# Gated delta stage: one table set for the norm's logarithm and exponential, a repeated identity product, key products behind the updates

## The reference

```python
q, k, v = causal_conv_silu(x @ Wq.T), causal_conv_silu(x @ Wk.T) * scale, causal_conv_silu(x @ Wv.T)
a, beta = sigmoid(x @ Wa.T + ba), sigmoid(x @ Wb.T + bb)
def step(S, (qt, kt, vt, at, bt)):            # one token
    err = einsum('bhij,bhj->bhi', S, kt) - vt
    S = at[..., None] * S - bt[..., None, None] * (err[..., None] * kt[:, :, None, :])
    o = einsum('bhij,bhj->bhi', S, qt)
o = scan(step, zeros, 512 tokens)
o = (o - mean(o)) / sqrt(var(o) + eps) * ln_w + ln_b      # per head
layer = (o * sigmoid(x @ Wg.T)) @ Wo.T
```

## Time and profile before

| | us |
|---|---|
| three runs | 2849.22, 2838.45, 2849.55 (median 2849.22) |
| the profiled execution, its own time | 2847.4 |
| its span (first to last instruction) | 2845.6 |
| VectorE busy in the span | 2072.3 (73%) |
| TensorE busy in the span | 2388.4 (84%) |
| ScalarE busy in the span | 1626.4 (57%) |
| mean granted TensorE clock | 0.923 of full speed |

### The profile page before, as it was taken

One profiled execution on the slowest core, in us unless ns is written; L12 is line 12 of the kernel. 1 busy time (PEld: TensorE's weight loads), 2 busy tenths in 40 slices (PEclk: granted clock), 3 DMA queues, 4 the chain that ended last, 5 costly groups with the idle time before them and its releaser, 6 DMA issues. The chain is left out here.

```text
span 2845.6 us, 63751 instructions
## 1 busy us (share of the span) xinstructions
PE 2388.4 (84%) x25649; PEld 1591.6 (56%) x25701; DVE 2072.3 (73%) x3811; ACT 1626.4 (57%) x4119; POOL 263.7 (9%) x278
## 2 busy tenths in 40 slices
PE   6788888877888788887994999999997886999777
PEld 5666666666667666664442666666642322332376
DVE  6889998889889889882123777778726775886465
ACT  3656677666666766665234777777641113667344
POOL 0000000000000000000011101100002342110342
PEclk9889999889999989998996999999998998999889
DMA  5110111111011111002006999999510003231422
GB/s 185 32 32 17 32 32 32 32 32 30 19 32 32 32 32 30 19 17 71 0 12 173 236 249 227 232 241 233 127 37 0 0 0 103 54 88 24 172 71 65
DMA packets 205726, 219.48 MB, mean 77 GB/s; under 512 B 32966, under 2 KB 191446, under 8 KB 199990
## 3 DMA queue, kind: packets, MB, share of 16 engines
q1 hardware_dynamic: 203033, 210.44, 28.3%
q0 software_dynamic: 2400, 4.95, 0.5%
HBM read 137.96 MB, written 79.79 MB: 77 GB/s over the span
## 5 line engine op out<-in xcount | busy, mean ns | idle before, releaser
L2871 DVE TENSOR_REDUCE dl_ZO<-dl_XP 128x64 f32<-128x128 f32 (+6 forms) x448 | 219.7, 490 | 15.5
L1990 ACT ACTIVATE da_AB<-ps 128x384 f32<-128x384 f32 x256 | 124.7, 491 | 140.8 <-PE ps L1851 137.1
L2866 DVE TENSOR_TENSOR dl_XP<-dl_ZO,dl_G 128x128 f32<-128x128 f32 (+5 forms) x384 | 177.0, 461 | 13.2
L2000 ACT ACTIVATE da_E<-ps,da_top 128x512 f32<-128x512 f32 x256 | 176.2, 688 | 17.2 <-DVE da_top L2146 16.7
L2143 DVE TENSOR_TENSOR ps<-ps,da_window 128x192 f32<-128x192 f32 (+1 forms) x256 | 101.3, 396 | 116.3 <-PE ps L1874 112.0
L1470 DVE TENSOR_REDUCE ra_top<-ps 128x1 f32<-128x512 f32 x256 | 159.2, 680 | 36.2 <-PE ps L1236 22.8
L2146 DVE TENSOR_REDUCE da_top<-ps 128x1 f32<-128x512 f32 x256 | 176.9, 691 | 8.8
L2450 PE MATMUL ps<-dl_ST,ident 128*128 128x512 f32 x256 | 139.3, 672 | 46.0 <-ACT dl_Q L2638 46.0
L1370 ACT ACTIVATE ra_PT<-ps 128x512 f32<-128x512 f32 x256 | 136.0, 601 | 61.0 <-PE ps L1267 59.1
L1881 PE MATMUL ps<-ident,da_E 128*128 128x128 f32 x1024 | 168.7, 288 | 1.6 <-ACT da_E L2000 1.5
L2384 PEld LDWEIGHTS ps<-X,dl_taps_v 128*128 128x128 f32 x1088 | 145.5, 216 | 18.2 <-issue 12.9
(11 more groups left out here) (411 smaller groups left out, 5855.9 us busy)
## 6 DMA issues: line engine op xcount, KB each, us to landing
da_bands<-da_AB SPq DMA_DIRECT2D x128, 384.0 KB, 3.8
dl_Abc<-dl_ends SPq DMA_DIRECT2D x64, 512.0 KB, 6.2
da_window<-da_bands SPq DMA_DIRECT2D x128, 192.0 KB, 4.4
da_across<-da_bands SPq DMA_DIRECT2D x128, 192.0 KB, 4.5
da_parts<-da_split SPq DMA_DIRECT2D x64, 96.0 KB, 3.4
ra_parts<-ra_split SPq DMA_DIRECT2D x16, 384.0 KB, 3.5
rf_We<-in_rf_We SPq DMA_DIRECT2D x1, 4608.0 KB, 24.1
da_K<-da_parts SPq DMA_DIRECT2D x16, 256.0 KB
```

The source lines that it names most:

```text
L1990: eng.activation(AB[:, j % STAGES, h, :, :], ps[:, band_bank(v), 0:2 * BAND].rearrange("p (k x) -> p k x", k=2), ACT.Copy)\
L2000: eng.activation(E[:, U % 2, :], ps[:, score_bank(U), :], ACT.Exp, bias=top[:, u:u + 1], accum_out=total[:, m % 2, u:u + 1]).then_inc(s["e ...
L2866: link(eng.tensor_tensor(XP[:, :, :, SB - t:], seen.unsqueeze(1).to_broadcast([P, 2, I, t + 1]), G[:, x:x + 2, keys][:, ::-1, :].unsqueeze ...
L2871: link(eng.tensor_reduce(ZO[:, to:to + 1 + (2 * I - 1) * CH:CH].rearrange("p (k i) -> p k i", k=2), XP[:, :, :, SB - 1 - t:], AXX, ALU.add))
```

## The change

Four edits in the delta stage. (1) `deviation` asks for one table set that has both functions, and stands ahead of the copy of the values' first half rather than behind it. (2) `kept(2)` is issued five times more ahead of itself; each overwrites bank 0 with the same quarter, so what is computed stays. (3) In the second half's boundary the products of `LAST_KEYS` stand behind the updates rather than ahead of them. (4) On VectorE `prepare(n + 1, 1)` stands ahead of `gate_keys` and `residual` rather than behind them.

```diff
+    REPEATS = 5
@@ TensorE
-            def kept(r):
-                eng.matmul(ps[:, UPDATES[r], :], c.ident[:, :], quarters[:, r, :, :], start=True, stop=False)
+            def kept(r, alone=False):
+                eng.matmul(ps[:, UPDATES[r], :], c.ident[:, :], quarters[:, r, :, :], start=True, stop=alone)
@@ boundary
                 eng.wait_ge(s["wc"], 6 * n + 3 * e + 3)
                 eng.sem_inc(c.past, 1)
+                for g, k, h, r in itertools.product(range(GR), range(2), range(2), range(GR)):
+                    update(g, k, h, r)
                 if e == 1:
                     key_products(LAST_KEYS).then_inc(s["g"], 1)
-                for g, k, h, r in itertools.product(range(GR), range(2), range(2), range(GR)):
-                    update(g, k, h, r)
                 for r in range(GR):
                     next_start(r)
@@ one_pass
                 eng.wait_ge(s["evac"], (n + 1) * PROJ + 3)
+                for _ in range(REPEATS):
+                    kept(2, True)
                 kept(2)
                 boundary(n, 0)
@@ ScalarE
             def deviation(n):
+                eng.preload_act_table_set("natural_log_exp_and_others")
                 eng.wait_ge(s["var"], n + 1)
@@ one_pass
-                evacuate(n + 1, 1, 3)
+                evacuate(n + 1, 1, 2)
                 if not first:
                     deviation(n - 1)
+                evacuate(n + 1, 2, 3)
                 boundary(n, 0)
@@ VectorE, one_pass
                 end(n, 1, first)
+                prepare(n + 1, 1)
                 gate_keys(n + 1)
                 if not first:
                     residual(n - 1)
-                prepare(n + 1, 1)
                 begin(n + 1, 0)
```

## The result

The changed kernel takes **2826.07 us** in the median of six runs (2822.43 to 2827.16), the kernel before 2850.22 in its six (2838.45 to 2855.65): ratio 0.9914 [0.9897, 0.9931]. The forecast was 2838, the likeliest case being no measurable change; it is faster by 0.9%. The profiled execution took 2825.35 with a span of 2823.6, 22.0 us shorter than the span before.

What follows compares the result with a forecast made beforehand. VectorE was taken as the busiest engine in the delta stage, so only its waits count. Against the profiled 2847.4: -13.0 + 2.0 + 0.9 - 1.3 = -11.4, so 2836.0, on the median 2838 us; range 2812 to 2862.

Steps and rivals of the forecast that it cites:

- the sum of the first halves: First halves of passes 1 to 15: nine products of 0.89 us up to the transposes, a loss of 2 us in all.
- I leave it unchanged: First halves, transposes to `begin`: mean kept at 7.33 us; ends 14 us won or 27 us lost.
- the second halves: `W` to `begin` with key products moved behind the updates: 13 us won together, between 0 and 33.
- its cover by edit 4: Second halves on VectorE: scan and its product, 1.6 us, fill the wait of `gate_keys` for the later key products.
- The nine passes: Second halves at 8.47 us each from `W` to `begin`: at most 1.07 to win, 0.85 taken, 7.7 us in all.
- The seven: Second halves at 11.4 us with stalls on issue that stay: 1.08 us less 0.3 for delayed keys, 7 x 0.76 = 5.3 won.
- Pass 0: First half without a logarithm to wait for: TensorE idles 3.54 us, five products take 4.45, a loss of 0.9 us.
- Behind the last pass: After the last pass nothing hides the chain and VectorE waits for the exponential: one table load, 1.3 us, goes.
- the slow second halves heal: Rival, 24%: keys fill the hole in the seven slow second halves, TensorE's clock stays up, 20 us more won: 2818.
- The key move is worth nothing: Rival, 17%: instruction supply sets the burst's end in second halves, so `begin` waits as before: 2851.
- The first half turns slower: Rival, 12%: clock falls in updates and starts with transposes 8.0 us behind `kept(3)`; 9.12 us in all passes: 2865.
- The named set was used: Answers a rival, 3%: the set by name is not used on ScalarE, two loads stay, copy ends 1.3 later: 2839.

Runs made afterwards that it cites:

- the order of the tables alone: Kernel before with only deviation moved ahead of the values' copy, a table set each for logarithm and exponential: 2832.97 us, ratio 0.9967.
- the set alone: Kernel before with only the named table set for logarithm and exponential, deviation left behind the values' copy: 2846.67 us, ratio 0.9999.
- the 32 products at the start: Changed kernel plus 32 products of 32 columns on TensorE at the delta stage's start, results unread: 2831.84 us, ratio 0.9929.

## Why the prediction was wrong

**Where it failed.** The failed step is the sum of the first halves: a loss of 2.0 us stood there, and they won 9.3. Two terms carry most of that miss of 11.3. The price of a `kept`, 0.89 us, was read from a row of three; in a row of nine it is 7.73 / 9 = 0.86, so the fifteen stretches to the transposes take 4.1 us less than forecast. And the way behind the transposes, "I leave it unchanged", was put at nothing, as no row showed what a full queue does to it; it became 5.8 us shorter. The second miss, 7.6 us, is the second halves, and most of it is the stalling ones (below).

The reason that stood against a gain behind the transposes was that in the seven passes with a full clock up to the transposes that way was longer, not shorter. It was longer, but the clock was not why. In two of the seven the updates stand still for 2 us, on "issue" (timeline of TensorE in the kernel before):

```profile
933.84 0.21 PE L2464 MATMUL ps<-dl_WT,dl_KT 32*64 32x64 f32 x1 [2.05 <-issue]
...
1165.89 0.34 PE L2464 MATMUL ps<-dl_WT,dl_KT 32*64 32x64 f32 x6 [1.97 <-issue]
```

Their ways took 9.01 and 9.12 us; the second is the longest row. The other five took (53.50 - 18.13) / 5 = 7.07 in the mean, as the eight's 56.45 / 8 = 7.06, so these two stalls are the whole difference. So the rows spoke neither for nor against the clock, and the one opposing reason was a stall of another kind.

How much of the 5.8 us the clock gave stays open. The two stalls are 4.0 of it: in the changed kernel no first half stalls in its updates. Ten of its fifteen ways ran at a clock of 1.00, before two did; but three ran at 0.76 to 0.81, and the mean rose only from 0.92 to 0.94. In the profiles in which TensorE's queue reaches past `W` in every one of these halves, the fifteen ways sum to 106.8 to 110.0 us without repeats (four kernels) and to 104.1 to 108.0 with five or eight (four kernels), 1.8 us less in the mean.

The rule weighed there, to leave TensorE no idle gap ahead of a burst (the Trainium skill, "TensorE: Matmul & The Clock Gate", section "HAM oscillation — how this bites in real kernels"), agrees in direction with the kernels in which there is such a gap: 8.43 us at a clock of 0.55 with it, 6.94 to 7.16 at 0.94 to 0.97 with repeats in its place. It does not explain the miss. In the kernel before, TensorE's queue reached past `W` in each of these halves, by 0.5 to 4.1 us, and it does so in the changed one; the order of the tables alone opens the gap, and what that costs lay in no row.

**Term by term**, forecast against the changed kernel's stretches:

- *First halves*, +2.0 forecast, -9.3 measured. The part up to the transposes was to grow by 2.0 and shrank by as much, 117.95 to 115.90, as nine products take 7.73 us and not 8.0. The way behind them, left at nothing, gave 109.95 - 104.14 = -5.8. The remaining 1.5 is 15 x 0.1 us that `kept(3)` starts earlier against `W` (5.92 us ahead of it, before 5.82).
- *Second halves*, -13.0 forecast, -20.6 measured. The move of 1.08 us and its cover by edit 4 were right, and both fell away as forecast where edit 4 was left out. The nine passes gave what was forecast: ten good ones now take 7.56 us, 0.9 less each. The seven were sized too carefully: six passes still stall, but take 9.94 and not 11.37, 1.4 less where 0.76 was forecast (1.08 less 0.3 is 0.78; the slip is 0.1 us in all), and one pass fewer is of that kind, which comes with the repeats: with edits 3 and 4 alone there are seven. One of the six, on TensorE (`W` at 492.37):

```profile
495.50 0.45 PE L2399 MATMUL ps<-dl_kqN,dl_kkN 64*64 64x64 f32 x8
497.77 0.74 PE L2399 MATMUL ps<-dl_kqN,dl_kkN 64*64 64x64 f32 x18 [1.82 <-issue]
...
501.90 0.59 PE L2446 MATMUL ps<-dl_kqN,dl_ST 64*64 64x32 f32 x25 [1.73 <-issue]
```

  The stall ends 5.4 us behind `W`, where it ended before too; but by then the updates are through, and in five of the six it hits the key products. `gate_keys` waits for those, 1.82 us here, which is a part of the 8.1 us above, and `begin` for 0.94. The granted clock, which fell behind the stall in all seven before, fell in one of the six.
- *Pass 0*, +0.9 forecast, -0.4 measured: there was no delay. `W` came 8.21 us behind `kept(3)` and not 6.99 (in the runs it is 6.9 to 8.4, with or without repeats), and the transposes still follow it by 0.15.
- *Behind the last pass*, -1.3 forecast, about -0.1 measured. The load went, but the variance that it waits beside ran longer. Timeline of TensorE, then VectorE:

```profile
1269.91 3.78 PE L2507 MATMUL ps<-dl_Q,dl_sums 128*128 128x512 f32 x4 [4.17 <-ACT dl_gate L2634]
...
1276.11 1.28 DVE L2895 SCALAR_TENSOR_TENSOR dl_D<-ps,dl_vec,dl_Q 128x1024 f32<-128x1024 f32 x1 [14.41 <-ACT dl_Q L2645]
```

  3.78 us after 4.17 idle; before, the same four took 1.98 after 2.29 idle. VectorE waits 14.41, before 14.48.

The four make -30.4 where -11.4 stood. The later layers gave back 8.5 of it in the profiled execution, which is why the miss of the whole is smaller than that of the stage.

**The rivals.** The one called "the slow second halves heal" had the size of the stage nearly right and the sign of its reason: with the keys in the hole the clock rose to 1.00. But the stalls stayed, as its counterargument said. Sixteen times the shift of 1.08 us is 17.3 of the 20.6; what the clock gave beside it no run separates. "The key move is worth nothing" fell with edits 3 and 4 alone, though it describes edit 3 alone. "The first half turns slower" fell in five repeats and came true in eight, by the delay and not by the clock. The named set was used, and is worth nothing by itself.

**The sum of the parts** in medians: edit 1 alone gives 13.7 us, edits 3 and 4 alone 9.3, together without repeats 20.6. The repeats add nothing to that at five, and some 23 us at two (2825.80 against 2803.06, whose runs of the kernel before lie 1 us apart). Put together the other way, edits 1 and 2 (5.9) and edits 3 and 4 (9.3), the parts fall short of the changed kernel's 24.2; the intervals of the three ratios are too wide to call that an effect.

**The signs that it named.** The way from transposes to `begin` in the first halves moved by 0.39 us in the mean, not by more than 1, and `gate_keys` waits in five passes, not in most: neither of the two signs of being wrong showed. `begin`'s wait tells more, 29.4 us where about 50 was forecast.

**Where the stalls on issue fall** can be read from the traces. In the kernel before and the six others that add no instruction to TensorE, the updates or key products of second halves stall in the same passes, 1, 3, 4, 6, 9, 12 and 15 (five of these with the set alone), in whichever order they stand; with repeats, or with the 32 products at the start, in others. Counted in order over all of TensorE's records (products, weight loads and those of its sequencer), the stalls on issue of more than 1 us lie whole multiples of 256 records apart: 264 of the 270 in the delta stages of the thirteen profiles do, to within 3 records. So "the instructions, not their order" was right, and so was it that twenty more a pass move the places.

**Not settled:** why only some of those places stall (some 20 of more than 100 in a stage), what the clock gave in either kind of half, and the 8 us of the later layers. Edit 4 without edit 3, and two repeats without the key products' move, were not tried.

## What to carry to other kernels

Ahead of a burst that waits for another engine, filling the wait with products kept TensorE's clock up here (0.97 against 0.55 in the mean), but every product beyond the operand's arrival is plain delay: size the filler by the gap in the timeline, and try one less and one more. Before a slow stretch is taken as evidence against a clock effect, look inside it for a stall that has nothing to do with the clock. When a product is moved behind others, the instruction that waits for it needs something moved ahead of itself, or the wait only changes its name.

## What the runs showed of the hardware

- After 2.61 us without work a stretch of 8.41 us ran wholly at the lower level of TensorE's clock; after 0.75 us one of 6.88 ran wholly at the full one. The length of the gap does not decide it alone: with the order alone, two of fifteen ways ran wholly at the full level after gaps of 1.72 and 1.84 us and others mostly at the lower one after 1.54, and in the kernel before seven of fifteen passes kept the full clock through the 3.06 us wait for the logarithm.
- TensorE stalls for 1 to 2.3 us on "issue" inside bursts of small products, with nothing in the profile that it waits for: in the updates or key products of six or seven of sixteen second halves in the kernel before, the changed one and that of edits 3 and 4 alone. Those stalls end 4.9 to 5.7 us behind `W` in all three (others fall into the starts); which products are hit there changes with the order. They lie whole multiples of 256 of TensorE's records apart.
- Sixteen table loads of 1283 ns less, where ScalarE waits anyway, changed nothing (the named set alone, 0.9999 [0.9974, 1.0024]); logarithm and exponential moved ahead of the copy that waits, with two loads of their own still, gave all of edit 1 (0.9967 against 0.9956).
